# One pair of shared-expert matmuls ahead of the router's ranks, and one silu ahead of a weight conversion

## The reference

```python
x = x + attention(layernorm(x), ctx)
xf = layernorm(x).reshape(N, D)                 # N = 2048, D = 256
logits = xf @ gate_w.T                          # E = 8 experts
topk_logits, topk_idx = top_k(logits, 2)
topk_w = softmax(topk_logits)
for e in range(E):                              # HALF = 384
    y = (silu(xf @ wg[e].T) * (xf @ wu[e].T)) @ w_down[e].T
    out += comb[:, e] * y                       # comb: topk_w, or 0
shared = (silu(xf @ sg_gate.T) * (xf @ sg_up.T)) @ sg_down.T
return x + shared + out
```

## Time and profile before

| | |
|---|---|
| Median of 3 runs | 508.62 us (508.53 to 511.54) |
| Profiled execution | 509.08 us, span 507.3 us |
| TensorE, matmul | busy 458.8 us, 90% |
| TensorE, weight load | 318.4 us, 63% |
| VectorE | 309.2 us, 61% |
| ScalarE | 210.1 us, 41% |
| GpSimd | 193.1 us, 38% |
| Mean granted TensorE clock | 0.964 of full speed |

### The profile page before, as it was taken

One profiled execution on the slowest core, in us unless ns is written; L12 is line 12 of the kernel. 1 busy time (PEld: TensorE's weight loads), 2 busy tenths in 40 slices (PEclk: granted clock), 3 DMA queues, 4 the chain that ended last, 5 costly groups with the idle time before them and its releaser, 6 DMA issues.

```text
span 507.3 us, 10169 instructions
## 1 busy us (share of the span) xinstructions
PE 458.8 (90%) x3098; PEld 318.4 (63%) x3099; DVE 309.2 (61%) x651; ACT 210.1 (41%) x419; POOL 193.1 (38%) x204
## 2 busy tenths in 40 slices
PE   7668999999999999988789599999999999999993
PEld 6444444564447444463356366499999999999852
DVE  4975656647574756546765696865555555555437
ACT  1235566616564375616862352522232232232210
POOL 4130336305441245301411000225667676676420
PEclk9976999999999999999979799999999999999997
DMA  8933121332224121310197910113444444444379
GB/s 265 262 90 121 34 91 43 96 120 68 68 73 130 67 84 43 103 76 2 39 369 268 396 22 0 42 33 44 72 74 65 74 69 65 75 69 67 40 190 337
DMA packets 45574, 53.84 MB, mean 106 GB/s; under 512 B 7760, under 2 KB 41872, under 8 KB 44912
## 3 DMA queue, kind: packets, MB, share of 16 engines
q1 hardware_dynamic: 34320, 39.77, 23.8%
q0 software_dynamic: 7488, 10.31, 12.7%
q10 hardware_dynamic: 3744, 3.47, 2.3%
HBM read 27.09 MB, written 13.67 MB: 80 GB/s over the span
## 4 chain that ended last, share of the span: by engine, by line
PE 68%; ACT 10%; DVE 9%; DMA 6%; issue 5%; SPq 1%; DVEq 0%; ACTq 0%; POOLq 0%
PE set_a L618 7%; PE set_b L648 6%; ACT attention L1060 5%; PE set_a L912 5%; PE set_a L913 5%; PE set_a L911 5%; PE set_a L842 5%; PE set_a L669 4%; PE set_b L638 4%; PE set_b L852 3%; DVE attention L1292 3%; PE set_b L930 3%; PE set_a L823 3%; PE set_b L931 3%; PE set_b L932 3%
## 5 line engine op out<-in xcount | busy, mean ns | idle before, releaser
L1292 DVE TENSOR_REDUCE attention<-set_a 128x2 f32<-128x1024 f32 (+2 forms) x96 | 96.0, 1042 | 32.3 <-PE set_a L620 30.4
L1060 ACT ACTIVATE attention<-set_b 128x512 f32<-128x512 f32 (+1 forms) x176 | 88.5, 571 | 60.5 <-PE set_b L638 48.0
L525 POOL TENSOR_SCALAR_AFFINE_SELECT attention<-attention 128x512 f32<-128x512 f32 x64 | 40.8, 649 | 120.8 <-ACT attention L1060 120.8
L584 POOL DMA_INDIRECT sum_rows<-moe,token_of x39 | 61.8, 1585 | 43.9 <-issue 29.6
L638 PE MATMUL set_b<-attention 99*128 99x512 bf16 (+3 forms) x256 | 60.2, 309 | 12.2 <-ACT attention L1060 9.9
L618 PE MATMUL set_a<-attention 96*128 96x512 bf16 (+3 forms) x256 | 63.7, 314 | 5.5 <-DVE attention L1292 3.7
L576 POOL DMA_INDIRECT e_x<-normed_rows,token_of x39 | 39.4, 1010 | 65.6 <-DVE token_of L1493 39.2
L1161 ACT ACTIVATE moe<-set_a 128x384 f32<-128x384 f32 x39 | 19.1, 490 | 104.9 <-PE set_a L913 99.7
L1518 DVE TENSOR_TENSOR moe<-set_a,moe 128x384 f32<-128x384 f32 x39 | 21.7, 558 | 62.7 <-issue 33.0
L618 PEld LDWEIGHTS set_a<-attention 96*128 96x128 bf16 x256 | 25.8, 101 | 47.3 <-DVE attention L1292 16.9
L911 PE MATMUL set_a<-wup_hi,e_xT_hi 128*128 x156 | 53.0, 340 | 0.0
(11 more groups left out here) (166 smaller groups left out, 841.9 us busy)
## 6 DMA issues: line engine op xcount, KB each, us to landing
attention<-attention SPq DMA_DIRECT2D x182, 64.0 KB, 2.6
wup<-in_wupT SPq DMA_DIRECT2D x2, 3072.0 KB, 13.9
sum_rows<-attention SPq DMA_DIRECT2D x2, 2048.0 KB, 13.3
wup<-sum_rows SPq DMA_DIRECT2D x8, 512.0 KB, 6.9
attention<-in_ctxT SPq DMA_DIRECT2D x7, 512.0 KB, 6.2
w_down<-in_wdnT SPq DMA_DIRECT2D x3, 1024.0 KB, 4.9
x_res<-in_x SPq DMA_DIRECT2D x4, 512.0 KB, 7.1
out<-x_res ACTq DMA_DIRECT2D x8, 256.0 KB, 4.0
```

The costliest lines, as they stand in the source:

```text
L584: g.indirect_dma_start(acc[i], bass.IndirectOffsetOnAxis(token_of[:, t:t + 1], 0), e_y[:, t % 2, :], None, compute_op=ALU.add).then_inc(ad ...
L1060: nc.scalar.activation(pT[k][:, h:h + heads, :], bank(par)[:, 0:heads * (S - k * P)], ACT.Exp).then_inc(b_free, 1)
L1292: v.tensor_reduce(dst, src, AX.X, ALU.max, negate=True).then_inc(a_free, 1)
```

## The change

Pair 1 of batch 0 (`shared_up(0, 1, 2)`) is issued ahead of the rank matmuls, behind a wait for `lg_read` that is new on TensorE; only pair 2 stays behind the ranks. On ScalarE the silus of batch 0 stand together, ahead of the wait for the up weights and the first four conversions; before, the first conversion stood between the second and the third silu. Nothing is computed that was not computed before.

```diff
--- before.py
+++ after.py
@@ -866,6 +866,9 @@
             pe.wait_ge(lt_read, 2)
             logits_t(B - 1).then_inc(logits_full, 1)
 
+            pe.wait_ge(lg_read, 1)
+            shared_up(0, 1, 2)
+
             pe.wait_ge(sel_ready, 1)
             rank = Bk[:, 2, 0:TE].rearrange("p (t e) -> p t e", e=E)
             mm(rank, beforeb[:], selb, start=True, stop=False, skip_group_check=True)
@@ -875,7 +878,7 @@
             for t in range(T):
                 last = mm(Bk[:, 3, 0:E], onesb[:], selb[:, t, :], start=t == 0, stop=t == T - 1)
             last.then_inc(rank_full, 1)
-            shared_up(0, 1)
+            shared_up(0, 2)
             pe.wait_ge(rank_read, 2)
             shared_down(0)
             shared_up(1)
@@ -1135,12 +1138,10 @@
                 for i in pieces:
                     copy(piece(wup_hi, i), piece(wup, i)).then_inc(up_hi, 1)
 
-            shared_silu(0, 0)
-            shared_silu(0, 1)
+            for m in range(M):
+                shared_silu(0, m)
             act.wait_ge(ld_up, DMA * C)
-            hi_parts(range(0, 1))
-            shared_silu(0, 2)
-            hi_parts(range(1, EARLY))
+            hi_parts(range(0, EARLY))
             for m in range(M):
                 shared_silu(1, m)
             act.wait_ge(lists_ready, 1)
```

## The result

| | before | after |
|---|---|---|
| Median, 6 runs each | 508.71 us (508.50 to 511.54) | 505.91 us (505.42 to 506.49) |
| Profiled execution | 509.08 us, span 507.3 | 505.84 us, span 504.1 |
| Mean granted TensorE clock | 0.964 | 0.977 |

The ratio of the times is 0.9932, 95% interval 0.9910 to 0.9955. By the medians the changed kernel is 2.8 us faster; 505.8 was forecast. The interval alone would allow anything from 2.3 to 4.6 us. All of it is under 1%, and counts as the same by the bound that the prediction set.

A forecast was written before the change was run, and what follows sets the result against it. TensorE was taken as the bound, with 4.36 us idle ahead of the ranks and a lowered clock. Down would start 3.74 us earlier but wait for h(0,2), ending 2.84 us earlier: 505.8 us, range 505.0 to 508.2.

The forecast's parts named there:

- The moved pair is free: TensorE ahead of the ranks: the pair of m=1 fits the 4.36 us idle time, costing 0 to 0.1 us, taken as 0.
- Pair 2 waits for h(0,0): TensorE behind the ranks: pair 2 idles 1.3 to 1.9 us until h(0,0), held by ScalarE's 1.28 us table load and silu.
- The clock: TensorE around the ranks: granted clock 1.00 from 288 to 296, so pair 2 takes 3.43 us.
- Rival A: Clock falls while pair 2 runs on TensorE: gain only 2.1 us (506.5) or 0.3 us (508.3); chance 0.18.
- Rival B: Clock stays low through pair 2 into down: with 9 us of it 0.8 us late, 509.4; chance 0.03.
- h(0,2) holds down: Down matmuls: part three waits 0.9 us for VectorE's h(0,2), ending at 297.94 instead of 300.78.
- Silu(0,2) ahead of the conversions costs nothing: ScalarE: first conversion starts at 292.7 instead of 292.86; cost 0, bounds 0 and 0.5 us.
- It lasts: Behind down: the 2.84 us survive through batch 1, the lists and the experts' start; h(1,0) is ready only just in time.
- rival C: Experts' start: if VectorE's lo parts held still, the gain is capped at 1.1 us of slack, 507.5; chance 0.08.
- Rival D: Down matmuls: if h(0,2) did not hold them, the full 3.74 us are gained, 504.9; chance 0.04.
- The number: Whole kernel: 2.84 us earlier, 505.8 us against the median of 508.62.

The follow-up runs named there:

- e1: The changed kernel with ScalarE's old order (first conversion between second and third silu), so only the pair is moved: 505.99 us, 0.9942 of the kernel before.
- e4: The changed kernel with silu(0,0) ahead of the router's exp on ScalarE, one more table load: 505.82 us, 0.9933 of the kernel before.
- e3: The kernel before with a useless stand-in for the moved pair, four added matmuls ahead of the ranks: 507.54 us, 0.9966 of the kernel before.
- e2: The kernel before with only ScalarE's new order, three silus and then four conversions: 509.42 us, 0.9995 of the kernel before.
- e7: The changed kernel with VectorE's h(0,2) ahead of the one-hot operation L1462: 506.53 us, 0.9945 of the kernel before.
- e8: The changed kernel with silu(0,0) ahead of the exp, h(0,2) ahead of L1462, h(1,0) ahead of the second hot-slot group: 504.28 us, 0.9905 of the kernel before.
- e5: The changed kernel run once more, unaltered, beside later experiments: 506.26 us, 0.9935 of the kernel before.
- e6: Repeat of e4, the changed kernel with silu(0,0) ahead of the exp: 505.76 us, 0.9928 of the kernel before.

## Why the prediction was right, by its steps

- *The moved pair is free.* Right: the pair starts 0.34 us behind the start of the copy (forecast 0.35), runs for 3.71 us and ends 0.27 us ahead of the ranks. e1 shows that it is free even where the clock falls inside it, as long as the clock is back for the ranks.
- *Pair 2 waits for h(0,0).* Right, 1.56 us (1.3 to 1.9 forecast), and e4 shows what holds h(0,0), the table load and the first silu: with them out of the way 1.3 us more go. The Trainium skill (ScalarE: Activation LUTs, section What ACT_TABLE_LOAD costs) adds a drain of 1.38 us to a switch of tables; the changed kernel has 1.28 us of load and the silu 0.01 us behind it, and in e4 the exp's table is loaded at 283.00 directly behind a silu that started at 282.39. The measurement decides.
- *The clock.* Right in the stretch, where it stayed at 1.00. e3 gives its share, 1.93 us, which the prediction had not set apart. Rival A, a fall while pair 2 runs, was seen in none of the seven profiles of kernels with the moved pair. That is one profile of each kernel and two of the changed one and of e4; what the clock did at this place in the other executions isn't known. The fall in e1 is of the kind that rival A described, a stretch with pauses paid for in dense work, only one pair earlier, where it is harmless. The Trainium skill (TensorE: Matmul & The Clock Gate, section A second HAM failure mode: psum-queue depth-cycling) tells of a kernel in which short, frequent idle times between groups of matmuls made the clock swing between its two levels; e1 fits that (0.51 from 281.2 to 284.7), the six other profiles of kernels with the moved pair don't show it there, with the same idle times. Rival B, the slower one, would have needed it twice over.
- *h(0,2) holds down.* Right, and right in time: part three starts 14.78 us behind the copy (295.58 - 280.80), as forecast (296.21 - 281.43). The idle time ahead of it is 0.63 us instead of 0.9 for two reasons: pair 2 took 3.54 us (287.80 to 291.34) and not 3.43, and idle time counts from the end of the last record, some 0.16 us behind the point where the next matmul could have started. Neither moves the sum. What does is part three itself, 1.83 us (295.58 to 297.41) instead of 1.73: batch 1 at 16.61 us, forecast 297.94 - 281.43 = 16.51. That is the 0.1 us by which the forecast of 2.84 was too high.
- *Silu(0,2) ahead of the conversions costs nothing.* Right, by e1 and e2.
- *It lasts.* Right: the lists, and the first expert matmul, each 2.73 us nearer to the copy, so rival C falls. The third pair of batch 1 found h(1,0) there (22.41 + 0.69 us behind the copy, the pair at 23.48), by less than 0.4 us; e7 shows how little that is.
- *Rival D* was too good to be had by itself. The prediction gave it 3.74 us if h(0,2) did not hold down; e7 took that hold away and got 0.2 us, because h(1,0) is next. With h(1,0) moved too, the whole hold pays: e8 has the lists 0.90 us ahead of e4.
- *The number.* 2.84 us were forecast, 2.74 found in the stretch and 2.80 between the medians. That the medians come so close is in part luck: the executions of one kernel scatter by a microsecond and more. By the profiled executions alone it would have been 509.08 - 505.84 = 3.24 us; the 0.63 us ahead of the copy are in that, and are not the change's.

## What to carry to other kernels

An idle time of TensorE can cost beyond itself, in the work behind it, if the clock falls in it: filling these 4.36 us gave 2.74 us, and 1.93 of them could be had even with useless work. Filling it doesn't make sure that the clock stays up (e1), but there the fall came where nothing waited for TensorE. Work moved into such a gap leaves the place where it stood uncovered, so look up what it had been hiding there (a table load, one silu and h(0,0), then one VectorE operation) and move that next. Where gains are below the scatter of whole executions, measure distances from a fixed event just ahead of the edit.

## What the runs showed of the hardware that was not expected

- The clock went down in the midst of dense matmuls (e1, from 281.2 to 284.7), after a stretch with 2.65 us busy of 4.20, and stayed up in seven other profiles (the change, e3 to e8) whose work in that stretch is the same or nearly so.
- A pair that starts behind a wait takes 0.10 us longer than one in a row: 1.82 us instead of 1.72 for its first group (287.80 to 289.62 in the changed kernel), in every profile where the clock was up. It isn't the wait alone: in e3 the pair directly behind the ranks has no idle time ahead of it and takes 1.80 us (287.31 to 289.11).
- The time at which the program reaches the router scattered by 2.1 us between ten profiles of kernels whose work doesn't differ up to there, and it goes with the granted clock in the first 50 us and from 253 to 263. From the copy to the first expert matmul the two kernels that were profiled twice (the change and e5, e4 and e6) repeat to 0.02 us; behind it the ten profiles take 173.3 to 174.1 us.
